# Delta-rule attention and slot mixture: the masked matrix stored whole by column block in one transfer, and two neighbouring steps moved

## What is computed

```python
def step(S, ins):
    q_t, k_t, v_t, a_t, b_t, g_t = ins
    trans = a_t * (I - b_t * k_t k_t^T)
    S = S @ trans + b_t * (v_t k_t^T)
    o = (q_t @ S) * g_t
x = x + (o @ Wo + bo)
```

## Time and profile before

| | us |
|---|---|
| runs before (3) | 1237.17 median, 1233.4 to 1241.47 |
| the profiled execution: its time | 1239.12 |
| its span, first to last instruction | 1237.3 |
| PE busy | 1130.7 (91%) |
| DVE busy | 936.0 (76%) |
| ACT busy | 735.5 (59%) |
| POOL busy | 305.6 (25%) |
| q1, the queue of SP's DMAs, share of 16 DMA engines | 24.5% |

### The profile page before, as it was taken

How to read it: one execution, slowest core, us unless ns; L and a number is a source line. 1 busy time by engine, 2 the same in 40 slices (tenths; PEclk the granted TensorE clock), 3 DMA queues, 4 the chain that set the end, 5 groups by cost and what they waited for, 6 DMA issues and landing times.

```text
span 1237.3 us, 27045 instructions
## 1 busy us (share of the span) xinstructions
PE 1130.7 (91%) x8600; PEld 861.7 (70%) x8600; DVE 936.0 (76%) x2195; ACT 735.5 (59%) x1385; POOL 305.6 (25%) x373
## 2 busy tenths in 40 slices
PE   4589888889898987899999999999999999999998
PEld 2367776777677766458678568688468688477687
DVE  4678787888777764799757799767798766998665
ACT  3435555556555543568766378765478755487854
POOL 2536555455555551100002000002000012000012
PEclk9689999999999998999999999999999999999999
DMA  5112223322222224323238111237020337000155
GB/s 183 36 36 63 70 75 92 99 70 69 73 73 69 69 81 104 94 70 63 63 73 162 47 35 35 74 77 162 32 49 21 86 80 150 26 1 1 18 108 131
DMA packets 179119, 90.36 MB, mean 73 GB/s; under 512 B 117280, under 2 KB 170528, under 8 KB 179040
## 3 DMA queue, kind: packets, MB, share of 16 engines
q1 hardware_dynamic: 171984, 71.74, 24.5%
q0 software_dynamic: 5792, 17.05, 4.8%
q10 hardware_dynamic: 1264, 0.53, 0.2%
HBM read 38.42 MB, written 25.69 MB: 52 GB/s over the span
## 4 chain that ended last, share of the span: by engine, by line
PE 58%; DVE 16%; issue 12%; ACT 6%; DMA 5%; POOL 1%; SPq 1%; DVEq 0%; ACTq 0%; POOLq 0%
PE m_wide L1998 14%; PE m_wide L1881 8%; PE m_wide L1975 7%; PE m_wide L1961 7%; DMA Mrep<-M_dram 5%; DVE m_Dm L1581 3%; PE a_bank L1216 3%; DVE m_El L1589 2%; PE m_wide L1986 2%; ACT m_Eh L1764 2%; DVE cmax L1552 2%; PE m_wide L1935 2%; PE a_bank L1180 2%; PE a_bank L1090 1%; ACT kh_ L894 1%
## 5 line engine op out<-in xcount | busy, mean ns | idle before, releaser
L1519 POOL DMA_DIRECT2D out_dram<-m_o x64 | 35.4, 553 | 627.3 <-DVE m_o L1703 624.5
L1935 PE MATMUL m_wide<-m_X,m_Eh 128*128 128x257 f16 (+1 forms) x1024 | 171.5, 273 | 2.6 <-DVE m_El L1589 2.3
L1881 PE MATMUL m_wide<-seT,XT 128*128 128x512 f16 x672 | 147.3, 379 | 0.9 <-issue 0.8
L1998 PE MATMUL m_wide<-m_Ph,m_Th 128*128 128x257 f16 x512 | 140.4, 274 | 4.3 <-DVE m_Pl L1628 4.3
L1935 PE MATMUL m_wide<-m_X,m_El 128*128 128x257 f16 (+1 forms) x512 | 139.7, 273 | 0.0
L1998 PE MATMUL m_wide<-m_Ph,m_Tl 128*128 128x257 f16 x512 | 139.4, 272 | 0.0
L1998 PE MATMUL m_wide<-m_Pl,m_Th 128*128 128x257 f16 x512 | 139.1, 272 | 0.0
L1881 PEld LDWEIGHTS m_wide<-seT,XT 128*128 (+1 forms) x672 | 65.5, 98 | 78.6 <-ACT L L1737 1.5
L1935 PEld LDWEIGHTS m_wide<-m_X,m_Eh 128*128 128x128 f16 x1024 | 99.2, 98 | 20.7 <-DVE m_El L1589 3.8
L1737 ACT COPY L<-m_wide 128x512 f32<-128x512 f32 (+1 forms) x112 | 65.1, 584 | 78.5 <-PE m_wide L1881 77.6
L1757 ACT ACTIVATE m_E<-m_Dm,m_eshift 128x512 f32<-128x512 f32 x128 | 92.5, 722 | 23.5 <-DVE m_Dm L1581 22.5
(11 more groups left out here) (197 smaller groups left out, 2702.9 us busy)
## 6 DMA issues: line engine op xcount, KB each, us to landing
L<-in_L_attn_x_dram SPq DMA_DIRECT2D x16, 512.0 KB, 6.8
Mrep<-M_dram SPq DMA_DIRECT2D x32, 256.0 KB
x_dram<-x SPq DMA_DIRECT2D x16, 512.0 KB, 6.4
m_X<-X_dram SPq DMA_DIRECT2D x128, 64.0 KB, 1.8
m_x1t<-x_dram POOLq DMA_DIRECT2D x32, 256.0 KB, 3.5
out_dram<-m_o POOLq DMA_DIRECT2D x64, 128.0 KB, 2.5
X_dram<-Xh SPq DMA_DIRECT2D x16, 256.0 KB, 2.3
X_dram<-Xl SPq DMA_DIRECT2D x16, 256.0 KB, 2.3
```

The source lines that it names most:

```text
L1881: last = pe.matmul(lg[t % 4], XT[:, sx * KD + k, bass.ds((4 * g + t) * P, P)], seT[:, ss, k, z * HS:(z + 1) * HS], start=(c == 0), stop=(c ...
L1935: last = pe.matmul(acc[v][q], e[t % 4][:, qs], X[:, sx, bass.ds(4 * g + t, 1), 0:XW].rearrange("q a n -> q (a n)"), start=first and e is E ...
L1998: last = pe.matmul(co[p], a, pp[:, e, 0:XW], start=(c == 0), stop=(c == 3 * NS - 1))
```

## The change

The masked matrix M is kept with its column block outermost, `[128, 8, 4, 16]` (block, batch, column in the block) in place of `[128, 4, 128]`. `blocks_out` becomes one DMA that stores all of M (256 KB, in runs of 64 elements, 256 bytes) where eight DMAs of 4 KB each stored the diagonal blocks in runs of 64 bytes. `M_dram` is larger, and `blocks_in` reads the same diagonal blocks from it with a stride of 144 rows from one block to the next, still in two transfers. `cut` reads M through the permuted pattern. The last doubling's quarter of M is copied into a new tile `Mhalf` by a new GpSimd instruction (`half_cut`, 64 partitions x 256 elements) behind the two cuts and ahead of GpSimd's `residual`; PE's last `products` reads this copy and waits for moff_ok, which now counts 3 a chunk, in place of M_ok. On SP `store_low(i)` moves from the end of step i to step i+1, behind `blocks_in` and ahead of `store_x1` (in step 14 it stays at the end, and the one of chunk 15 comes behind all steps); SP's loop starts one pair of steps later. On DVE the last `doubling(i+1, 2)` moves from behind column s = 0 to ahead of the loop (in step -1 also ahead of the slots' scaling).

```diff
-        M = two("M", [P, B, P])
+        M = two("M", [P, NBK, B, BS])
+        Mhalf = two("Mhalf", [HP, B, HP])
...
-        def steps(eng, step, looped=NCH // 2 - 2):
+        def steps(eng, step, looped=NCH // 2 - 2, first=0):
...
             def blocks_out(c, q):
                 sp.wait_ge(M_ok, c + 1)
-                for e in range(NBK):
-                    sp.dma_start(M_dram[e],
-                                 M[q][e * BS:(e + 1) * BS, :, e * BS:(e + 1) * BS]).then_inc(M_out, 16)
+                sp.dma_start(M_dram[0:NBK * P * B * BS].rearrange("(e p f) -> p e f", e=NBK, p=P),
+                             M[q][:, :, :, :].rearrange("p e b t -> p e (b t)")).then_inc(M_out, 16)
...
                 for rows_in, s in ((Mrep_in, 0), (Mrep_late, HROWS)):
                     sp.dma_start(Mrep[:, s:s + HROWS, :, :].rearrange("p s b t -> p (s b t)"),
-                                 M_dram[:, s:s + HROWS].rearrange("e (a s) b t -> e a (s b t)", a=1)
+                                 M_dram.rearrange("(e a f) -> e a f", e=NBK, a=1)
+                                 [:, :, s * B * BS:(s + HROWS) * B * BS]
                                  .broadcast_to([NBK, BS, HROWS * B * BS])).then_inc(rows_in, 16)
...
                 if live(i + 2):
                     blocks_in(i + 2)
+                if live(i - 1) and not (isinstance(i, int) and i == NCH - 1):
+                    store_low(i - 1)
                 if live(i):
                     store_x1(i)
...
-                if live(i):
+                if isinstance(i, int) and i == NCH - 2:
                     store_low(i)
-                if isinstance(i, int) and i == NCH - 2:
                     load_XT0(XT0_PARTS[0], XT0_PARTS[1])
 
-            steps(sp, step)
+            steps(sp, step, first=1)
+            store_low(NCH - 1)
             load_XT0(XT0_PARTS[1], NCH)
...
+            def half_cut(c, q):
+                pool.wait_ge(M_ok, c + 1)
+                pool.tensor_tensor(Mhalf[q][:, :, :].rearrange("p b (e t) -> p b e t", t=BS),
+                                   M[q][0:HP, NBK // 2:, :, :].rearrange("p e b t -> p b e t"),
+                                   pool_zeros[0:HP, :].rearrange("p (b e t) -> p b e t", e=1, t=1)
+                                   .broadcast_to([HP, B, NBK // 2, BS]), ALU.add).then_inc(moff_ok, 1)
...
                     cut(i + 3, r, 0)
+                    half_cut(i + 3, r)
                 if live(i + 3):
                     residual(i + 3, r)
...
                 if live(i + 3):
                     biases(i + 3, r, 0)
+                if live(i + 1):
+                    doubling(i + 1, r, 2)
                 if at == -2:
...
-                    if s == 0:
-                        if live(i + 1):
-                            doubling(i + 1, r, 2)
...
-                        last = pe.matmul(bank[4][HP:, bs], M[q][0:HP, b, HP:], ZT[0:HP, bs], start=True, stop=True)
+                        last = pe.matmul(bank[4][HP:, bs], Mhalf[q][:, b, :], ZT[0:HP, bs], start=True, stop=True)
...
-        M_dram = nc.dram_tensor("M_dram", (NBK, BS, B, BS), F32, kind="Internal").ap()
+        M_dram = nc.dram_tensor("M_dram", (NBK * (P + BS) * B * BS,), F32, kind="Internal").ap()
```

More of the change, by code:

```diff
@@ L239, in attention @@
         N_MIX = 6 * 16
-        def steps(eng, step, looped=NCH // 2 - 2):
-            for i in range(-4, 0):
+        def steps(eng, step, looped=NCH // 2 - 2, first=0):
+            for i in range(-4, 2 * first):
                 step(i, i % 2)
-            with eng.Fori(0, looped) as j:
+            with eng.Fori(first, looped) as j:
                 for q in range(2):
@@ L285, in blocks_out @@
                 sp.wait_ge(M_ok, c + 1)
-                for e in range(NBK):
-                    sp.dma_start(M_dram[e],
-                                 M[q][e * BS:(e + 1) * BS, :, e * BS:(e + 1) * BS]).then_inc(M_out, 16)
+                sp.dma_start(M_dram[0:NBK * P * B * BS].rearrange("(e p f) -> p e f", e=NBK, p=P),
+                             M[q][:, :, :, :].rearrange("p e b t -> p e (b t)")).then_inc(M_out, 16)
             def blocks_in(c):
-                out, used = value(sp, 16 * NBK * (c + 1)), value(sp, c)
+                out, used = value(sp, 16 * (c + 1)), value(sp, c)
                 sp.wait_ge(M_out, out)
@@ L444, in cut @@
                 at = C_MASK + n * P
-                pool.tensor_tensor(moff[q][:, n], M[q][:, :, :], over_batches(const[:, at:at + P]), ALU.mult)\
+                pool.tensor_tensor(moff[q][:, n].rearrange("p b (e t) -> p b e t", t=BS),
+                                   M[q][:, :, :, :].rearrange("p e b t -> p b e t"),
+                                   const[:, at:at + P].rearrange("p (a e t) -> p a e t", a=1, t=BS)
+                                   .broadcast_to([P, B, NBK, BS]), ALU.mult)\
                     .then_inc(moff_ok, 1)
+            def half_cut(c, q):
[4 more added lines that the diff above has]
+                                   .broadcast_to([HP, B, NBK // 2, BS]), ALU.add).then_inc(moff_ok, 1)
             def spread_blocks(c, q):
@@ L565, in system @@
                 if later(c, 2):
-                    dve.wait_ge(moff_ok, NCUT * (c - 1))
-                    dve.wait_ge(M_out, 16 * NBK * (c - 1))
-                dve.tensor_tensor(M[q][:, :, :], by_batch[6], gamb[q][:, :, :], ALU.mult).then_inc(M_ok, 1)
+                    dve.wait_ge(moff_ok, NLV * (c - 1))
+                    dve.wait_ge(M_out, 16 * (c - 1))
+                dve.tensor_tensor(M[q][:, :, :, :].rearrange("p e b t -> p b e t"),
+                                  by_batch[6].rearrange("p b (e t) -> p b e t", t=BS),
+                                  gamb[q][:, :, :].rearrange("p b (e t) -> p b e t", t=BS), ALU.mult).then_inc(M_ok, 1)
             def product(c, s):
@@ L1132, in products @@
             def products(c, q, n):
-                turned, made = value(pe, NLV * c + n + 1), value(pe, NCUT * c + NCUT - n if n < NCUT else c + 1)
+                turned, made = value(pe, NLV * c + n + 1), value(pe, NLV * c + (NCUT - n if n < NCUT else NLV))
                 pe.wait_ge(pool_consts, 1)
                 pe.wait_ge(ZT_ok, turned)
-                pe.wait_ge(moff_ok if n < NCUT else M_ok, made)
+                pe.wait_ge(moff_ok, made)
                 for b in range(B):
```

## The result

The changed kernel takes **1232.76 us** (median, 1229.98 to 1235.26), the kernel before 1236.49 (1231.87 to 1241.47) beside it: ratio 0.9967, 95% interval 0.9952 to 0.9982. That is 4 us where 29 were forecast, and outside the range. The profiled executions differ by 7.4 us (span 1237.3 and 1229.9).

What follows compares the result with a forecast made beforehand. In the attention, DVE's wait for Mrep, caused by SP's queue order and the slow eightfold store, was taken as the bound. -22.9 + 0.4 - 2.1 - 2.5 - 3.8 + 1.7 = -29.2 us, from 1237.17 to 1208.0; 8-in-10 range 1200 to 1219.

Steps and rivals of the forecast that it cites:

- The wait for Mrep: DVE's idle time ahead of its first read of Mrep goes in steps 1 to 12 of the attention: -22.9 us.
- The rest of 25.5 us: Product-to-product time of an attention step less its wait for Mrep: 25.54 us in step 4, 25.53 in step 0.
- Both edits are needed for a margin: SP's new order alone brings Mrep at 241.3 to 242.5 against a need at 242.3, so the single store is needed too.
- The wide store: SP's store of M as one transfer: issue about 0.65 us for 5.16, landing after 3.2 us, Mrep 3 to 4 us early.
- B: Rival: the store of M lands late, from 6.2 us on the wait comes back; 1222 us at 8 us; chance 0.07.
- C: Rival: slower than before, M's small packets need over 9 us to land; 1254 us at 11 us; chance 0.03.
- Copy on GpSimd: The 0.65 us copy, 0.5 covered, pushes kTg under DVE's Xl, costing 0.14 in 12 steps: +1.7 us, bounds 0 and 9.6.
- Rival A: Another wait, on PE or POOL, takes over in part on DVE: 1224 us in full, 1216 for half; chance 0.12.
- Doubling ahead of the loop: DVE's last doubling ahead of the column loop, its 0.3 us mostly covered at heads and before M: +0.4 us, bounds 0 and +4.2.
- Step -1: The doubling also passes the slots' scaling, so DVE's 1.97 us wait at the scores goes: -2.1 us, bounds 0 and -4.2.
- Step 13: Without keys and values on PE, the earlier doubling brings DVE's scores sooner: -2.5 us, between -1.5 and -3.5.
- Clock: PE's idle ahead of the updates shrinks below 0.5 us, so three clock falls in twelve steps go: -3.8 us, bounds 0 and -3.8.

Runs made afterwards that it cites:

- queries_late: The changed kernel with GpSimd's decayed_queries (qTg) moved behind output_norm in the same step, the copy left in place: 1228.5 us, ratio 0.991 to the kernel before.
- doubling_only: The kernel before with only the last doubling moved ahead of the column loop: 1230.31 us, ratio 0.9942 to the kernel before.

## Why the prediction was right or wrong, step by step

- *The wait for Mrep* (-22.9): right in mechanism and size for the wait by itself. It was gone from the profile, it came back with SP's old order, and SP's order alone gave 1208.31. The rest of 25.5 us under the wait was right too: 25.46 with the order alone, 25.5 with the doubling back.
- *"Both edits are needed for a margin"*: wrong. The eight stores with the new order leave the fetch 5.49 us, which was just the long end of the forecast's own 4.3 to 5.5. The wide store sends the fetch 6.32 - 2.63 = 3.7 us sooner behind the store's issue, and nothing uses that.
- *The wide store* (3.2 us to land): 2.6. The estimate of 2.6 by the Trainium skill, "SBUF — State Buffer", The DMA setup-cost knee, agrees with the trace. Of the rule of the Trainium skill, "DMA: Bandwidth & Descriptors", Specifications (at least 512 bytes a descriptor), the runs show little: 2.6 us in runs of 256 bytes against 2.4 in runs of 512. Rivals B and C fall. The lines of the page of the profile on DMA issues, answering to the earlier trace rows:

```profile
L<-in_L_attn_x_dram SPq DMA_DIRECT2D x16, 512.0 KB, 4.8
...
M_dram<-M_ SPq DMA_DIRECT2D x16, 256.0 KB, 2.6
```

- *Copy on GpSimd* (+1.7): this is the step that failed. The copy's duration (0.65, measured 0.61) and its cover (0.5, measured 0.52) were right. The push of `kTg` (0.15, measured 6.68 - 6.49 = 0.19) came out near by luck: the copy alone pushes it by 0.05 at most (6.50 to 6.54 us behind M), and the 0.19 needs the doubling ahead of the loop, a meeting of two terms that the forecast summed as if each stood alone. The price was wrong altogether: it was "the push", 0.14 a step, as if Xl waited only for the end of `kTg`. That is what it costs where nothing stands behind `kTg` (`queries_late`, 1.51 - 1.34 = 0.17). Here it waits for `qTg` as well, 1.40 a step, in nine steps 12.6 us and above the bound of 9.6, which took the copy at its longest and priced it as a push too. The forecast had looked at `kTg` in the earlier trace rows and not at the 2.26 us of `qTg` behind it, where the same shape takes 1.27 in `kTg`: the trace showed already that one of the two engines had to stand there, and which one was a matter of 0.2 us. Rival A had the right engine and the right rule, with too small a price: 1224 at its far end, where 1232.76 was measured. Two of the forecast's own signs of being wrong came: products over 26.5 us apart and an Xl of over 1.6 us.
- *Doubling ahead of the loop* (+0.4): 25.65 us a step without Xl's excess, against the rest of 25.53, is 1.4 in twelve steps, and 0.2 a step against the order alone. The cover at `heads` and ahead of M didn't hold in full. Its larger cost was the second push.
- *Step -1* (-2.1): failed. From its first product to that of step 0 it takes 107.16 - 78.36 = 28.80 us, before 105.05 - 76.20 = 28.85. DVE's wait at the scores went, but PE's idle stretch of 4.2 us moved from the updates to the queries, and the clock fell beside it as before. And the step ahead of it grew: the DVE subtraction of `w1s` came while POOL's `residual` ran and stood until `kTg` and `qTg` had passed, 5.72 us where before it took 4.01. This goes with the copy and not with the doubling: in all six kernels that have the copy behind the cuts `w1s` takes 5.7 to 6.8 us, with the copy alone too (5.78), and in the others 3.9 to 4.3. DVE, POOL and PE after, then DVE and POOL before:

```profile
62.15 2.35 POOL L414 TENSOR_TENSOR L<-L,bo 128x1024 f32<-128x1024 f32 x1
63.39 5.72 DVE L710 TENSOR_TENSOR w1s<-L,w1s 128x2048 f16<-128x2048 f32 x1
64.46 1.27 POOL L436 TENSOR_TENSOR kTg_<-kT,gbc_ 128x512 f32<-128x512 f32 x1
...
82.77 0.61 PE L1105 MATMUL a_bank<-L,wqg_h 128*128 128x512 f16 x1 [4.32 <-DVE L L555]
```

```profile
62.42 4.01 DVE L694 TENSOR_TENSOR w1s<-L,w1s 128x2048 f16<-128x2048 f32 x1
64.24 3.32 POOL L433 TENSOR_TENSOR kTg_<-kT,gbc_ 128x512 f32<-128x512 f32 x1
```

- *Step 13* (-2.5): right, and small. PE's updates wait 0.51 us and run 1.16, DVE's scores come without a wait, against the earlier trace rows; from the product of step 12 to the end it is -4.3. Timeline:

```profile
460.46 1.16 PE L1195 MATMUL a_bank<-X,Z_ 128*128 128x128 f32 x8 [0.51 <-DVE Z_ L624]
...
465.35 0.69 DVE L641 TENSOR_TENSOR PT<-a_bank,gamb_ 128x512 f32<-128x512 f32 x1
```

- *Clock* (-3.8): right in size for what the kernel before loses, wrong in cause and sign for the change. Less their wait for Mrep, its steps take 25.5 us, and 27.0, 26.9 and 26.8 in the three with a fall: 4.0 in all. With SP's order alone these falls are gone, together with PE's idle ahead of the updates. In the changed kernel that idle went too, and yet there are three falls, and longer ones (0.50 where 0.72 was, over the 6 us shown above). DVE's waits for the scores, on which the term rested, hardly changed (2.6 to 1.9 us from 120 to 450) and are the smaller part; before the product stand the larger ones, which Mrep's wait had hidden. The three falls cost 7.6. In none of the kernels with steps of 25.4 to 26.0 us did the clock fall within steps 1 to 12; it did in the two that have Xl at 2.74. In these, PE waits 1.3 us ahead of its transposes for the DVE subtraction that stands behind Xl, in steps with a fall and without; with a short Xl it doesn't. That the standing Xl brings the falls about is likely by this, not shown: the kernel before has falls without it, and PE waits of 0.9 to 1.6 us (`doubling_only`) and 0.8 to 0.9 (`queries_late`) in every step brought none. What sets a fall off stays open.

Of the 21.8 us missing: Xl 12.6 - 1.7 = 10.9; the clock 7.6, where the forecast left no fall in these steps; the doubling 1.4 - 0.4 = 1.0; step -1 2.1; `w1s` 1.7; the end gives back 1.8. The sum is 21.5. Xl, `w1s` and the steps' lengths are read from the trace; the split of a long step into clock and rest is a subtraction.

## What to carry to other kernels

When an edit puts work on GpSimd, list each DVE instruction with two SBUF inputs that runs at the same time as GpSimd's, and look at what stands *behind* the GpSimd instruction in flight: the price of losing the ports is the rest of the one in flight and the whole of what is queued behind it, and it can turn on a few tenths of a us. Two edits that each fit into the same idle gap may not fit together. An instruction that takes more time than the same shape elsewhere (here `qTg`, 2.26 against 1.27) marks such a place before any edit. And try a change of order in a queue by itself first: here the order of two transfers alone took 1241.71 to 1208.31 us, and no other part was shown to add to it.

## What the runs showed of the hardware

- Which waiting instruction has the ports next changes with when the DVE instruction came: having come 0.80 to 0.85 us into a GpSimd instruction of 1.27 it let the next GpSimd one pass (2.73 to 2.78 us), having come 0.98 to 1.03 us into it it went first (1.33 to 1.36 us), in one and the same kernel too. Later is not always better: into the GpSimd `residual` of 2.35 us `w1s` came after 0.24 to 0.60 us and went first in eight kernels; after 0.13 to 0.15 us (three kernels) or 1.17 to 1.24 us (three) it let both of the next pass. What decides is not shown.
- The exclusion holds for small instructions too: a DVE product of 128x60, 0.20 us by itself, took 1.07 beside a GpSimd multiplication, and 0.38 beside the 0.61-us copy.
- 256 KB written in runs of 256 bytes landed in 2.6 us, against 2.4 for the same amount in runs of 512 (Xh and Xl, after). The load of x landed in 4.8 us in place of 6.8 once it left 8.4 us behind the fetch of the blocks and not 2.3.
- With the order alone, where the store of Xl is issued 2.0 us behind the fetch of the blocks, it landed in 5.0 us in place of 2.3.
- PE, busy 6.00 of 6.00 us, had the lower clock all along after the change. Its matmuls take longer at that level (the last doubling's 1.12 us for 0.67), so that this share is in part the clock's effect.
